# A chain of attention and feed-forward layers on one core: one low part placed ahead of a rotation, projections sent one slot later, and row sums by four narrow products

## The chip, the cores and the metric

The kernel runs on one core of a Trainium2 chip. The metric is the device time of one execution in microseconds (us). Each run of the kernel before is one such time; the profile is one further execution, recorded by the hardware profiler, with its own time and its own span from the first to the last instruction.

## What is computed

Four residual layers over x of shape (4, 1024, 256), each with a layernorm in front:

```python
x = x + attention0(layernorm(x))   # 8 heads of 64, keys and values from a 64-wide latent
x = x + ffn0(layernorm(x))         # 256 -> 1024 gated (silu), 1024 -> 1024 gelu, 1024 -> 1024 gelu, 1024 -> 256
x = x + attention1(layernorm(x))   # 16 heads of 16, rotary positions on q and k
x = x + ffn1(layernorm(x))         # 256 -> 768 gated (silu), 768 -> 256
# attention: softmax(q k^T * scale) v, and then the output projection
```

All is float32. A value that has to stay exact goes through TensorE in two parts: a high part rounded to fp32r, and a low part that holds what the rounding left. A low part is one elementwise subtraction.

## The kernel before

Two programs run one after the other. `attention_a` computes the first attention; `ffn_attention_ffn` computes the other three layers in one overlapped program. Each engine runs a written list of instructions in order; semaphores tie the lists together.

**First attention.** The work is cut into NU = 32 units (a batch, a pair of heads, a half of 512 queries), each of 8 steps of 128 keys; two steps make one turn, so that a unit has four turns j = 0 to 3. Within a turn TensorE computes row maxima (tile a_X, in three banks psX), scores (a_S), and the weighted values of the turn before (a_O, four products on 64 output partitions each). ScalarE takes the exponential (a_P), VectorE reduces the maxima (a_mraw) and adds some of the a_P tiles (a_accd), GpSimd adds the others (a_accp) and joins them. Once a unit, in turn j = 1, `sums(u - 1)` (L986 to L996) multiplies a block of ones with a_accd: two products, one for each head, each of 64 output partitions and 512 columns in full float32, so that the sum of the exponentials of each query stands 64 times in a bank. `keep_sums` (L591) copies the whole bank to `total`, `move_sums` (L468) spreads one row of each head with two transfers over the 128 partitions of `rcol`, 8 numbers each, `invert` (L740) takes the reciprocal in turn j = 2, and `move_inverse` sends it back through DRAM. The last unit keeps the wide form, because its reciprocals are taken straight from the bank.

**The program of the other three layers.** The first feed-forward works on NB = 8 batches k of 512 tokens; a batch has 64 slots H, and in each slot TensorE gets 5 or 6 of the 352 products of the batch (`slice_at`, `product`, L2005). They are grouped by output tile: 64 products make the 16 tiles gate and up, then come 8 tiles `("hidden", k, 0, m)`, 8 tiles `("hidden", k, 1, m)` and 2 tiles down, with 16 products a tile. ScalarE applies gelu twice for a hidden tile, once to a high part (act1h or act0h) and once to a full copy (m_xf); GpSimd's `low(key)` (L1926 to L1930) subtracts them into the low part (act1l or act0l). A product of the next layer reads high and low parts in turn over the 8 tiles m of the layer before; in `product` it waits by `s_lo`. So the first tile of the second hidden layer needs, with its fifteenth product, the low part of `("hidden", k, 0, 7)`, whose own last product stands in slot 34 of the batch.

Beside it runs the start of the second attention: for the batch kk = k - 1 that is through the feed-forward, `PROJECT` puts four projections (six products each, key and query in two halves) in slots 26, 30, 34 and 38, and `VALUES` four value products in slots 28, 32, 36 and 40. All use the one bank m_X. A projection is copied by ScalarE (`keep_projection`, tile m_qk, L1690), shuffled out of the bank by VectorE (`swap`, L1839), which waits for the end of the rotation before, rotated by GpSimd (`rotate`, three operations, L1938, L1940, L1942, result m_t1), rounded by ScalarE into the first half of the tile m_comp (`send_high`, L1696), its low part subtracted by GpSimd into the second half (`send_low`, L1947), and written to DRAM by SyncE's queue (`send`, L1513). There is one m_comp: `send_high` waits until the transfer of the projection before has landed (`s_sent`), and `rotate` waits for its low part.

What sets the order within a slot H is the loop of each engine. GpSimd: low parts of tiles up, `send_low`, output low parts, `rotate`, low parts of tiles hidden, the power of a layernorm. ScalarE: `keep_projection`, `send_high`, then the tiles that ended in this slot. `send_high` and `send_low` stand three slots after their projection, `send` five slots after it. START = 512 is the slot in which the second attention's scores begin; its first row maxima come 24 slots earlier, and the fourth query tile of the attention (index 3, used first by unit u = 5) is the tile m_comp, cleared by GpSimd's `fill_queries` at START + 46 and fetched at START + 48.

Of the kernel before, what the change touches and what calls it, by code (L numbers as in the profile page):

```python
# [10 lines left out]
ACT = mybir.ActivationFunctionType  # L11
# [113 lines left out]
def mm(pe, out, lhsT, rhs, start=True, stop=True):  # L125
    return pe.eng.matmul(out, lhsT, rhs, start=start, stop=stop, skip_group_check=True)  # L126
# [117 lines left out]
def attention_a(nc, x_in, x_out, weights, scales, c_ident, scratch, wtiles, wcopy, dtiles, dcopy, shared):  # L244
# [7 lines left out]
    NU = B * UB  # L252
# [93 lines left out]
    with ExitStack() as ctx:  # L346
# [15 lines left out]
        wo = [p.sb(f"wo{i}", [128, NG, 256], F32R) for i in range(2)]  # L362
        accd, accp = [p.sb(f"accd{i}", [128, NH, 512]) for i in range(2)], p.sb("accp", [128, NH, 512])
        mrow = [p.sb(f"mrow{i}", [NH * 4, 128], F32R) for i in range(2)]
        total = p.sb("total", [128, 512])
        wraw = p.sb("wraw", [128, NG, 320])
        rinv = [p.sb(f"rinv{i}", [128, 512]) for i in range(2)]
        ON = [p.sb(f"ON{i}", [128, NG, T]) for i in range(2)]
# [41 lines left out]
        def bank(key):  # L410
            return psX[:, X.slot(key), :]
# [24 lines left out]
        def sync(eng):  # L436
# [31 lines left out]
            def move_sums(u):  # L468
                sp.wait_ge(*X.emptied(("sums", u)))
                sp.wait_ge(s_rout, 16 * u)  # L470
                for h in range(NH):
                    sp.eng.dma_start(rcol[64 * h:64 * h + 64, :], total[64 * h:64 * h + 1, :]).then_inc(s_total, 16)

            def move_inverse(u):
                sp.wait_ge(s_rcol, u + 1)
# [65 lines left out]
        def scalar(eng):  # L541
# [49 lines left out]
            def keep_sums(u):  # L591
                key = ("sums", u)
                act.wait_ge(*X.filled(key))
                act.wait_ge(s_total, 32 * u)
                act.eng.activation(total[:, :], bank(key), ACT.Copy).then_inc(X.free(key))

            def out_high(b, t):
                i = out_index(b, t)
# [74 lines left out]
        def vector(eng):  # L673
# [64 lines left out]
                    dve.eng.tensor_tensor(acc[:, :, :], acc[:, :, :], P[n % NP][:, :, :], ALU.add).then_inc(s_addd)  # L738

            def invert(u):  # L740
                dve.wait_ge(s_total, 32 * (u + 1))
                dve.eng.reciprocal(rcol[:, :], rcol[:, :]).then_inc(s_rcol)

            def out_low(b, t):
# [163 lines left out]
        def tensor(eng):  # L908
# [77 lines left out]
            def sums(u):  # L986
                key = ("sums", u)
                pe.wait_free(X, key)
                pe.wait_ge(s_addp, 5 * u + (5 if u < NU - 1 else 4))
                pe.wait_ge(s_addd, 2 * u + 2)  # L990
                terms = (accd[u % 2],) if u < NU - 1 else (accd[u % 2], accp)
                for i, acc in enumerate(terms):
                    for h in range(NH):
                        ins = mm(pe, bank(key)[64 * h:64 * h + 64, :], ones[:, :], acc[:, h, :], i == 0, i == len(terms) - 1)
                ins.then_inc(X.full(key))

            def way(i):
# [97 lines left out]
def ffn_attention_ffn(nc, x_in, x_mid, x_att, x_out, attn, wcopy, dcopy, c_rope, scratch, shared):  # L1095
# [19 lines left out]
    NU = B * UB  # L1115
# [125 lines left out]
    def x_of(H, name):  # L1241
        x = x_at(H) if H >= 0 else None
        return x if x and x[0] == name else None
# [11 lines left out]
        return None  # L1255

    def send_at(H):
        return x_of(H - 5, "project")

    def send_high_at(H):  # L1260
        return x_of(H - 3, "project")

    def x_order():
        return [x_at(H) for H in range(END) if x_at(H)]
# [38 lines left out]
    with ExitStack() as ctx:  # L1303
# [155 lines left out]
        def sync(eng):  # L1459
# [144 lines left out]
            for H in range(END):  # L1604
                (k, s), h = divmod(H, SLOTS), H - START
                for i in weights_done_at(H - 1):
                    load_weights(i + 3)
                if H == LAST - 12:
                    load_norm(norm_of["d", 1])
                if H > LAST and H % 8 == 7 and last_at(H)[0] + 2 < NB:  # L1610
                    load_norm(norm_of["d", last_at(H)[0] + 2])
                for x in residuals_at(H - 1):
                    store(x)
                if x_of(H - 1, "rows"):
                    move_rows(x_at(H - 1)[1])
                if x_of(H - 1, "values"):
                    send_values(*x_at(H - 1)[1:])
                if send_at(H):
                    send(*send_at(H)[1:])
                gi, u = (h + 32) // 32, (h + 38) // 16  # L1620
                if (h + 32) % 32 == 0 and 0 <= gi < B * NG:
                    fetch_key(gi)
                if (h + 32) % 16 == 0 and 0 <= (h + 32) // 16 < 6:
                    fetch_query((h + 32) // 16)
                if (h + 38) % 16 == 0 and 6 <= u < NU:
                    fetch_query(u)
                if ended_unit_at(H, SUMS) is not None:
                    move_sums(ended_unit_at(H, SUMS))
                if ended_unit_at(H, INVERSES) is not None:
                    move_inverses(ended_unit_at(H, INVERSES))  # L1630
                    move_heads(ended_unit_at(H, INVERSES))
                if ended_unit_at(H, SPREAD) is not None:
                    spread_inverses(ended_unit_at(H, SPREAD))
                b, t = (h + 12) // 128, (h + 12) % 128 // 2
                if h % 2 == 0 and 0 <= b < B and t < NT:
                    fetch_values(b, t)
                if s == C_LOAD and 1 <= k <= NB:
                    load_norm(norm_of["c", k - 1])
                if s == B_LOAD and 1 <= k and k + 1 < NB:
                    load_norm(norm_of["b", k + 1])  # L1640
                if s == 46 and 1 <= k < NB:
                    load_rope(k)
                if H == START + 2:
                    for i in range(3):
                        load_last_gates(i)
                if H == START + 80:
                    load_last_back()
                if H == D_LOAD:
                    load_norm(norm_of["d", 0])
                for x in residuals_at(H + 7):  # L1650
                    if x[0] == "out":
                        load_residual(x)
                for x in residuals_at(H + 3):
                    if x[0] != "out":
                        load_residual(x)
# [266 lines left out]
        def gpsimd(eng):  # L1922
# [49 lines left out]
                    pool.eng.memset(f32(comp[64 * h + 32:64 * h + 64, :, :]), 0.0).then_inc(s_qfill)  # L1972

            for H in range(END):
                if H == START + 46:
                    fill_queries()
                for key in ended_at(H - 1):
                    if key[0] == "up":
                        low(key)
                if send_high_at(H):  # L1980
                    send_low(*send_high_at(H)[1:])
                if split_at(H):
                    out_low(*split_at(H))
                if ended_unit_at(H, NORMALISE) is not None:
                    b, g, half = unit(ended_unit_at(H, NORMALISE))
                    if g % 2:
                        normalise(b, g // 2, half)
                if x_of(H, "project"):
                    rotate(*x_at(H)[1:])
                for key in ended_at(H):  # L1990
                    if key[0] == "hidden":
                        low(key)
                if last_pair_at(H - 1):
                    last_low(*last_pair_at(H - 1))
                if norm_at(H) and norm_at(H)[1] == 0:
                    norm.power(pool, norm_at(H)[0])
                if H == C_PIECES[1]:
                    norm.power(pool, norm_of["c", NB - 1])
                if H == D_PIECES[1]:
                    norm.power(pool, norm_of["d", 0])  # L2000
# [268 lines left out]
```

## Time and profile before

| | us |
|---|---|
| median of 3 runs | 2463.66 |
| lowest and highest run | 2458.45, 2463.93 |
| time of the profiled execution | 2452.89 |
| span of the profiled execution | 2451.1 |
| mean granted clock of TensorE | 0.987 |

| engine | busy us | share of the span |
|---|---|---|
| TensorE (PE) | 2352.9 | 96% |
| its weight loads (PEld) | 1458.9 | 60% |
| VectorE (DVE) | 1508.7 | 62% |
| ScalarE (ACT) | 1352.8 | 55% |
| GpSimd (POOL) | 1044.7 | 43% |

A record of the profile gives the start of an instruction in us from the span's start, its duration, engine, line, operation, and the tiles that it writes and reads. Idle time stands in brackets with the engine and line that ended it. Matmuls are pipelined: the recorded duration of one reaches into the next, so what one occupies is read from the distance between two starts. The span falls into three stages: the first attention up to about 800 us, the first feed-forward from about 855 to 1570 us, and the second attention with the last feed-forward behind it.

### The profile page before, as it was taken

How to read it: one execution, taken by the hardware profiler on the slowest of the kernel's cores; microseconds unless marked ns; L12 is line 12 of the kernel's file. 1: busy time of each engine (PE TensorE's matmuls, PEld its weight loads, DVE VectorE, ACT ScalarE, POOL GpSimd, SP SyncE). 2: the span in 40 equal slices, each digit the busy share in tenths (PEclk: the TensorE clock that was granted, in tenths of full speed). 3: DMA queues.
4: the chain of work that ended last, by engine and by line, in shares of the span. 5: the costliest groups of instructions: out<-in, count | busy, mean ns of one | idle time of the engine just before them, and what ended most of it. 6: DMA issues, size and time to landing. Idle time of an engine off the chain costs nothing. (4 is left out here: it accounts for less than half of the span.)

```text
span 2451.1 us, 38790 instructions
## 1 busy us (share of the span) xinstructions
PE 2352.9 (96%) x15141; PEld 1458.9 (60%) x15141; DVE 1508.7 (62%) x1934; ACT 1352.8 (55%) x1787; POOL 1044.7 (43%) x674
## 2 busy tenths in 40 slices
PE   6989999999999899999999999999999999999899
PEld 4545555555555687877877877544444444444598
DVE  6887777777774223322222222689989989889364
ACT  3555555554454444444444444378878778778643
POOL 1656766766677346556456456130010000000354
PEclk8999999999999999999999999999999999999999
DMA  1211321221212455555555555533432333332232
GB/s 50 71 68 53 96 78 53 96 74 48 73 42 68 139 170 172 170 181 182 175 180 183 169 180 181 148 96 73 90 88 64 89 77 73 90 79 50 61 113 82
DMA packets 157702, 259.02 MB, mean 106 GB/s; under 512 B 37872, under 2 KB 98160, under 8 KB 157168
## 3 DMA queue, kind: packets, MB, share of 16 engines
q1 hardware_dynamic: 157520, 256.53, 34.9%
q8 instruction: 122, 2.00, 0.3%
q14 instruction: 60, 0.49, 0.1%
HBM read 206.52 MB, written 60.68 MB: 109 GB/s over the span
## 5 line engine op out<-in xcount | busy, mean ns | idle before, releaser
L1825 DVE TENSOR_REDUCE m_mraw<-m_R 128x2 f32<-128x1024 f32 x512 | 622.5, 1221 | 70.2 <-PE m_R L126 58.5
L1676 ACT ACTIVATE m_P<-m_R 128x1024 f32<-128x1024 f32 x512 | 524.1, 1025 | 151.6 <-PE m_R L126 151.3
L581 ACT ACTIVATE a_P<-a_S 128x1024 f32<-128x1024 f32 x256 | 248.9, 1024 | 208.3 <-PE a_S L126 208.3
L126 PE MATMUL m_O<-m_P,m_V 128*17 128x256 f32 x4096 | 330.5, 394 | 4.5 <-ACT m_P L1676 2.6
L1930 POOL TENSOR_TENSOR m_act0l<-m_xf,m_act0h 128x512 fp32r<-128x512 f32 x128 | 164.6, 1289 | 240.2 <-ACT m_xf L1738 136.3
L879 POOL TENSOR_TENSOR a_accp<-a_accp,a_P 128x1024 f32<-128x1024 f32 x96 | 250.9, 2614 | 15.2 <-ACT a_P L581 6.4
L126 PE MATMUL a_O<-a_P,a_V 128*64 128x512 f32 x1024 | 247.7, 605 | 4.5 <-ACT a_ON L589 4.5
L126 PE MATMUL m_R<-m_act0h,wt 128*128 128x512 f32 x640 | 251.4, 393 | 0.0
L712 DVE TENSOR_REDUCE a_mraw<-a_X 128x2 f32<-128x1024 f32 x164 | 200.0, 1219 | 82.9 <-PE a_X L126 82.9
L126 PE MATMUL m_R<-m_act0l,wt 128*128 128x512 f32 x640 | 250.4, 391 | 0.0
L126 PE MATMUL m_R<-m_act1h,wt 128*128 128x512 f32 x512 | 203.0, 397 | 12.3 <-POOL m_act1l L1930 12.3
L126 PE MATMUL m_R<-m_act1l,wt 128*128 128x512 f32 x512 | 203.6, 398 | 0.0
L126 PE MATMUL m_R<-m_Q,m_K 64*128 64x512 f32 x800 | 201.0, 499 | 2.3 <-DVE m_mraw L1825 2.0
L126 PE MATMUL m_R<-next_hi,wt 128*128 128x512 f32 x448 | 179.2, 400 | 13.8 <-issue 10.1
L126 PE MATMUL m_R<-m_K,m_Q 48*128 48x512 f32 x800 | 181.9, 450 | 4.3 <-ACT m_P L1676 2.2
L1954 POOL TENSOR_TENSOR m_ON<-m_ON,m_yt 128x512 f32<-128x512 f32 x16 | 20.5, 1281 | 383.5 <-DMA m_yt<-inverses 383.5
L126 PE MATMUL m_R<-next_lo,wt 128*128 128x512 f32 x448 | 178.6, 399 | 0.0
L126 PEld LDWEIGHTS m_O<-m_P,m_V 128*17 128x17 f32 x4096 | 85.2, 120 | 140.8 <-issue 131.2
L126 PEld LDWEIGHTS m_R<-m_Q,m_K 64*128 64x128 f32 x800 | 74.8, 183 | 151.7 <-issue 122.3
L126 PEld LDWEIGHTS m_R<-m_act0h,wt 128*128 128x128 f32 x640 | 120.2, 188 | 26.8 <-POOL m_act0l L1930 2.1
L126 PEld LDWEIGHTS m_R<-m_act0l,wt 128*128 128x128 f32 x640 | 120.3, 188 | 24.4 <-issue 0.5
L126 PE MATMUL a_X<-a_Kh,a_Qh 64*128 64x512 f32 x496 | 113.6, 449 | 18.3 <-DVE a_mraw L712 10.8
(244 smaller groups left out, 4264.2 us busy)
## 6 DMA issues: line engine op xcount, KB each, us to landing
wt<-wcopy SPq DMA_DIRECT2D x176, 512.0 KB, 3.4
m_xres<-x SPq DMA_DIRECT2D x96, 128.0 KB, 3.0
m_K<-bounce_k SPq DMA_DIRECT2D x96, 128.0 KB, 5.2
m_ln_x<-x SPq DMA_DIRECT2D x23, 512.0 KB, 4.2
a_tile<-in_L_ffn_tiles SPq DMA_DIRECT2D x22, 512.0 KB, 4.7
wcopy<-in_L_ffn_tiles SPq DMA_DIRECT2D x22, 512.0 KB, 5.4
m_Q<-bounce_q SPq DMA_DIRECT2D x150, 64.0 KB, 2.3
x<-m_xres SPq DMA_DIRECT2D x64, 128.0 KB, 2.7
```

The lines of the kernel that those rows point to most:

```text
L126: return pe.eng.matmul(out, lhsT, rhs, start=start, stop=stop, skip_group_check=True)
L581: act.eng.activation(P[n % NP][:, :, :], psS[n % 2][:, :, :], ACT.Exp, scale=SCALE).then_inc(s_exp)
L712: dve.eng.tensor_reduce(mraw[u % 2][:, t, :], psX[:, first:first + 2, :], AX.X, ALU.max).then_inc(X.free(key))
L879: pool.eng.tensor_tensor(accp[:, :, :], accp[:, :, :], P[n % NP][:, :, :], ALU.add).then_inc(s_addp)
L1676: act.eng.activation(P[h % 4][:, :, :], pair(key)[:, :, :], ACT.Exp, scale=SCALE).then_inc(R.free(key))
L1825: dve.eng.tensor_reduce(mraw[u % 2][:, at, :], pair(key)[:, :, :], AX.X, ALU.max).then_inc(R.free(key))
L1930: pool.eng.tensor_tensor(act_buf[dst][1][:, m, :], xf[fs(key) % 2][:, :], f32(act_buf[dst][0][:, m, :]), ALU.subtract).then_inc(s_lo)
L1954: pool.eng.tensor_tensor(ON[:, f, cols], ON[:, f, cols], yt[half][:, :], ALU.mult).then_inc(s_norm[half])
```

## The change

In the first attention, the sums of 31 of the 32 units are made by four products of 32 output partitions and 256 columns; product i takes half of the queries of one head. The bank then holds 256 columns, `total` has half its width and its copy too, and one transfer takes the rows 0, 32, 64 and 96 in place of two transfers of one row each.

In the first feed-forward, `send_high`, `send_low` and `send` stand one slot later. In GpSimd's slot, the low part of the tile `("hidden", k, 0, 7)` comes ahead of the rotation. At the start of the second attention, m_comp is cleared at START + 48 and the query of unit 5 fetched into it at START + 50.

```diff
-                for h in range(NH):
-                    sp.eng.dma_start(rcol[64 * h:64 * h + 64, :], total[64 * h:64 * h + 1, :]).then_inc(s_total, 16)
+                sp.eng.dma_start(rcol[:, :], total[0:128:32, :]).then_inc(s_total, 16)
...
-                act.eng.activation(total[:, :], bank(key), ACT.Copy).then_inc(X.free(key))
+                act.eng.activation(total[:, :], bank(key)[:, 0:256], ACT.Copy).then_inc(X.free(key))
...
-                terms = (accd[u % 2],) if u < NU - 1 else (accd[u % 2], accp)
-                for i, acc in enumerate(terms):
-                    for h in range(NH):
-                        ins = mm(pe, bank(key)[64 * h:64 * h + 64, :], ones[:, :], acc[:, h, :], i == 0, i == len(terms) - 1)
+                if u < NU - 1:
+                    for i in range(4):
+                        ins = mm(pe, bank(key)[32 * i:32 * i + 32, 0:256], ones[:, 0:32], accd[u % 2][:, i // 2, 256 * (i % 2):256 * (i % 2) + 256])
...
     def send_at(H):
-        return x_of(H - 5, "project")
+        return x_of(H - 6, "project")
...
     def send_high_at(H):
-        return x_of(H - 3, "project")
+        return x_of(H - 4, "project")
...
-                if (h + 32) % 16 == 0 and 0 <= (h + 32) // 16 < 6:
+                if (h + 32) % 16 == 0 and 0 <= (h + 32) // 16 < 5:
                     fetch_query((h + 32) // 16)
+                if h == 50:
+                    fetch_query(5)
...
-                if H == START + 46:
+                if H == START + 48:
                     fill_queries()
...
+                awaited = [key for key in ended_at(H) if key[0] == "hidden" and key[2:] == (0, MT - 1)]
+                for key in awaited:
+                    low(key)
                 if x_of(H, "project"):
                     rotate(*x_at(H)[1:])
                 for key in ended_at(H):
-                    if key[0] == "hidden":
+                    if key[0] == "hidden" and key not in awaited:
                         low(key)
```

TensorE's list in the first attention, at one unit's sums (a_O the weighted values, a_accd the added exponentials, a_Kh and a_Qh the parts of keys and queries; the shape is that of the output):

```order
@@ -122,5 +122,5 @@
 L126 MATMUL a_X<-a_Kh,a_Qh 128x512 x2
 L126 MATMUL a_O<-a_P,a_V 64x512 x4
-L126 MATMUL a_X<-a_accd,a_ones 64x512 x2
+L126 MATMUL a_X<-a_accd,a_ones 32x256 x4
 L126 MATMUL a_X<-a_Kh,a_Qh 128x512 x2
 L126 MATMUL a_S<-a_Qh,a_Kh 128x512 x2
```

The sums stay between the weighted values and the maxima; four products stand where two were.

GpSimd's list in a batch of the first feed-forward, slots 30 to 38, before (m_act1l are low parts of the first hidden layer, m_act0l of the second, m_t1 and m_t2 the rotation, m_comp the low part of what is sent):

```order
L1938 TENSOR_TENSOR m_t1<-m_qk,m_rope 128x512
L1940 TENSOR_TENSOR m_t2<-m_t2,m_rope 128x512
L1942 TENSOR_TENSOR m_t1<-m_t1,m_t2 128x512
L1930 TENSOR_TENSOR m_act1l<-m_xf0,m_act1h 128x512
L193 TENSOR_TENSOR m_ln_rstd<-m_ln_ve,m_ln_minus_half 128x4
L1947 TENSOR_TENSOR m_comp<-m_t1,m_comp 128x512
L1938 TENSOR_TENSOR m_t1<-m_qk,m_rope 128x512
L1940 TENSOR_TENSOR m_t2<-m_t2,m_rope 128x512
L1942 TENSOR_TENSOR m_t1<-m_t1,m_t2 128x512
L1930 TENSOR_TENSOR m_act1l<-m_xf1,m_act1h 128x512
L1947 TENSOR_TENSOR m_comp<-m_t1,m_comp 128x512
L1930 TENSOR_TENSOR m_act0l<-m_xf0,m_act0h 128x512
```

And now:

```order
L1942 TENSOR_TENSOR m_t1<-m_qk,m_rope 128x512
L1944 TENSOR_TENSOR m_t2<-m_t2,m_rope 128x512
L1946 TENSOR_TENSOR m_t1<-m_t1,m_t2 128x512
L1934 TENSOR_TENSOR m_act1l<-m_xf0,m_act1h 128x512
L193 TENSOR_TENSOR m_ln_rstd<-m_ln_ve,m_ln_minus_half 128x4
L1951 TENSOR_TENSOR m_comp<-m_t1,m_comp 128x512
L1934 TENSOR_TENSOR m_act1l<-m_xf1,m_act1h 128x512
L1942 TENSOR_TENSOR m_t1<-m_qk,m_rope 128x512
L1944 TENSOR_TENSOR m_t2<-m_t2,m_rope 128x512
L1946 TENSOR_TENSOR m_t1<-m_t1,m_t2 128x512
L1934 TENSOR_TENSOR m_act0l<-m_xf0,m_act0h 128x512
L1951 TENSOR_TENSOR m_comp<-m_t1,m_comp 128x512
```

The last low part of the first hidden layer has passed the three operations of the rotation; the low part of the sent projection still stands ahead of both, but belongs to slot 34 now.

ScalarE's list in slots 33 to 38, before (m_qk is the copy of a projection, m_comp the high part of what is sent, m_act1h and m_xf the two outputs of a hidden tile):

```order
L1696 ACTIVATE m_comp<-m_t1 128x512
L1690 ACTIVATE m_qk<-m_X 128x512
L1737 ACTIVATE m_act1h<-m_R,scol 128x512
L1738 ACTIVATE m_xf1<-m_R,scol 128x512
L1703 ACTIVATE m_vstage0<-m_X 128x256
L1696 ACTIVATE m_comp<-m_t1 128x512
L1737 ACTIVATE m_act0h<-m_R,scol 128x512
L1738 ACTIVATE m_xf0<-m_R,scol 128x512
L1690 ACTIVATE m_qk<-m_X 128x512
```

And now:

```order
L1694 ACTIVATE m_qk<-m_X 128x512
L1700 ACTIVATE m_comp<-m_t1 128x512
L1741 ACTIVATE m_act1h<-m_R,scol 128x512
L1742 ACTIVATE m_xf1<-m_R,scol 128x512
L1707 ACTIVATE m_vstage0<-m_X 128x256
L1741 ACTIVATE m_act0h<-m_R,scol 128x512
L1742 ACTIVATE m_xf0<-m_R,scol 128x512
L1694 ACTIVATE m_qk<-m_X 128x512
L1700 ACTIVATE m_comp<-m_t1 128x512
```

The high part of a sent projection stood ahead of the next projection's copy and stands behind it now, directly ahead of the hidden tile that ends in slot 34.

## Rows read from the trace of the kernel before

**Rows 1.** The page: busy time, share and instructions of TensorE and its weight loads.

```profile
PE 2352.9 (96%) x15141; PEld 1458.9 (60%) x15141; DVE 1508.7 (62%) x1934; ACT 1352.8 (55%) x1787; POOL 1044.7 (43%) x674
```

**Rows 2.** Who TensorE waited for: total us, times, longest.

```profile
PE m_R L126 <- POOL m_act1l L1930: 12.3, 7, 1.9
...
PE m_X L126 <- DVE m_t L1839: 0.9, 1, 0.9
```

**Rows 3.** Stretches: busy PE, PEld, DVE, ACT, POOL, granted clock, DMA share, GB/s.

```profile
200.00:300.00 100.00, 99.98 (x626) 56.48 (x624) 74.51 (x85) 49.91 (x62) 70.76 (x31) 1.00 0.28 90
...
1045.92:1050.92 5.00, 5.00 (x15) 3.98 (x16) 0.59 (x2) 2.27 (x4) 3.11 (x3) 0.66 0.59 209
...
1236.07:1241.07 5.00, 5.00 (x23) 4.17 (x24) 0.74 (x2) 2.20 (x4) 4.11 (x4) 1.00 0.62 209
```

**Rows 4.** TensorE in order of time at the wait of batch k = 2.

```profile
1043.39 0.39 PE L126 MATMUL m_R<-m_act1h,wt 128*128 128x512 f32 x1
1043.62 0.39 PE L126 MATMUL m_R<-m_act1l,wt 128*128 128x512 f32 x1
1045.92 0.50 PE L126 MATMUL m_R<-m_act1h,wt 128*128 128x512 f32 x1 [1.91 <-POOL m_act1l L1930]
...
1047.31 0.63 PE L126 MATMUL m_X<-next_lo,m_wqh 128*128 128x512 f32 x1
1047.74 0.63 PE L126 MATMUL m_X<-next_hi,m_wql 128*128 128x512 f32 x1
```

**Rows 5.** The same wait in batches 4 and 5.

```profile
1236.07 0.50 PE L126 MATMUL m_R<-m_act1h,wt 128*128 128x512 f32 x1 [1.91 <-POOL m_act1l L1930]
1329.56 0.60 PE L126 MATMUL m_R<-m_act1h,wt 128*128 128x512 f32 x1 [1.91 <-POOL m_act1l L1930]
```

**Rows 6.** ScalarE, VectorE and GpSimd in order of time, batch 2, slots 30 to 38.

```profile
1031.91 0.60 ACT L1690 ACTIVATE m_qk<-m_X 128x512 f32<-128x512 f32 x1 [0.67 <-PE m_X L126]
...
1039.00 0.60 ACT L1690 ACTIVATE m_qk<-m_X 128x512 f32<-128x512 f32 x1 [1.31 <-PE m_X L126]
...
1039.64 0.74 DVE L1839 STREAM_SHUFFLE m_t<-m_X 128x512 f32<-128x512 f32 x1
...
1040.65 1.29 POOL L1938 TENSOR_TENSOR m_t<-m_qk,m_rope 128x512 f32<-128x512 f32 x1
1040.72 0.68 ACT L1738 ACTIVATE m_xf<-m_R,scol 128x512 f32<-128x512 f32 x1
...
1044.55 1.31 POOL L1930 TENSOR_TENSOR m_act1l<-m_xf,m_act1h 128x512 fp32r<-128x512 f32 x1
1045.70 0.63 ACT L1696 ACTIVATE m_comp<-m_t 128x512 fp32r<-128x512 f32 x1 [3.11 <-DMA bounce_q<-m_comp]
```

**Rows 7.** The transfers of the tile m_comp, from issue to landing.

```profile
DMA to landing us min/median/max: 2.1/2.6/5.6
```

**Rows 8.** ScalarE in batch 7, ahead of the copy of the last projection.

```profile
1521.77 0.63 ACT L1696 ACTIVATE m_comp<-m_t 128x512 fp32r<-128x512 f32 x1 [5.34 <-DMA bounce_q<-m_comp]
```

**Rows 9.** TensorE in the first attention at one unit's sums.

```profile
404.72 1.03 PE L126 MATMUL a_X<-a_accd,a_ones 128*64 128x512 f32 x4
...
405.68 0.50 PE L126 MATMUL a_X<-a_Kh,a_Qh 64*128 64x512 f32 x2
```

**Rows 10.** TensorE in the second attention: four narrow products, and what follows.

```profile
1900.99 0.64 PE L126 MATMUL m_O<-m_P,m_V 128*17 128x256 f32 x8
1901.57 0.49 PE L126 MATMUL m_R<-m_Q,m_K 64*128 64x512 f32 x2
```

**Rows 11.** Sums of an early unit, and a wait behind them.

```profile
94.69 1.03 PE L126 MATMUL a_X<-a_accd,a_ones 128*64 128x512 f32 x4
96.34 0.50 PE L126 MATMUL a_X<-a_Kh,a_Qh 64*128 64x512 f32 x2 [0.62 <-DVE a_mraw L712]
```

**Rows 12.** The query of unit 5: its fetch on the queue, and its first use.

```profile
1652.38 2.96 SPq L1536 DMA_DIRECT2D m_comp<-bounce_q  x6
...
1664.29 0.50 PE L126 MATMUL m_R<-m_K,m_comp 48*128 48x512 f32 x2
```

More of the change, by code:

```diff
@@ L364, in attention_a @@
         mrow = [p.sb(f"mrow{i}", [NH * 4, 128], F32R) for i in range(2)]
-        total = p.sb("total", [128, 512])
+        total = p.sb("total", [128, 256])
         wraw = p.sb("wraw", [128, NG, 320])
@@ L593, in keep_sums @@
                 act.wait_ge(*X.filled(key))
-                act.wait_ge(s_total, 32 * u)
-                act.eng.activation(total[:, :], bank(key), ACT.Copy).then_inc(X.free(key))
+                act.wait_ge(s_total, 16 * u)
+                act.eng.activation(total[:, :], bank(key)[:, 0:256], ACT.Copy).then_inc(X.free(key))
             def out_high(b, t):
@@ L740, in invert @@
             def invert(u):
-                dve.wait_ge(s_total, 32 * (u + 1))
+                dve.wait_ge(s_total, 16 * (u + 1))
                 dve.eng.reciprocal(rcol[:, :], rcol[:, :]).then_inc(s_rcol)
@@ L990, in sums @@
                 pe.wait_ge(s_addd, 2 * u + 2)
-                terms = (accd[u % 2],) if u < NU - 1 else (accd[u % 2], accp)
-                for i, acc in enumerate(terms):
-                    for h in range(NH):
-                        ins = mm(pe, bank(key)[64 * h:64 * h + 64, :], ones[:, :], acc[:, h, :], i == 0, i == len(terms) - 1)
+                if u < NU - 1:
+                    for i in range(4):
+                        ins = mm(pe, bank(key)[32 * i:32 * i + 32, 0:256], ones[:, 0:32], accd[u % 2][:, i // 2, 256 * (i % 2):256 * (i % 2) + 256])
+                else:
+                    for i, acc in enumerate((accd[u % 2], accp)):
+                        for h in range(NH):
+                            ins = mm(pe, bank(key)[64 * h:64 * h + 64, :], ones[:, :], acc[:, h, :], i == 0, i == 1)
                 ins.then_inc(X.full(key))
```

## The prediction

> **What bounds the kernel now.** I read the page first, for the engine that is busy all the time: TensorE, 2352.9 of 2451.1 us [rows 1]. A change pays here only if it takes work or waiting from TensorE. Next comes the table of who TensorE waited for. In the first feed-forward it names one thing: seven waits, 12.3 us together, each ended by GpSimd's line 1930, the low part of a first-hidden-layer tile; a single wait of 0.9 us on the shuffle of the projection bank stands beside it [rows 2]. Third, stretches of time, where the reader should look at the granted clock. A hundred us of the first attention hold 99.98 us of TensorE work at 1.00, while the 5 us behind the second of the seven waits have a clock of 0.66 [rows 3]. Last, the timelines of the engines, to see what the waiting product waits for.
>
> What one of the seven waits costs: the starts at 1043.39 and 1043.62 are 0.23 us apart, those at 1043.62 and 1045.92 are 2.30 apart, so 2.07 us are lost (the bracket calls 1.91 of them idle). Behind it the starts lie 0.43 us apart, for products that took 0.23 before [rows 4]: the clock is at 1.2 in place of 2.4 GHz. From batch 2's wait to batch 4's are 190.15 us, 95.08 a batch [rows 4, 5]; from batch 4's to batch 5's 93.49 [rows 5], and behind batch 4's the clock stayed at 1.00 [rows 3]. The half clock thus costs 95.08 - 93.49 = 1.6 us. The granted clock fell so behind five of the six waits of 1.91 us (the stretches behind batches 1, 3, 5 and 6 repeat the 0.66 of batch 2); the seventh, 12.3 - 6 x 1.91 = 0.8 us idle [rows 2], was too short.
>
> **The low part ahead of the rotation.** The awaited low part needs m_xf, ready at 1040.72 + 0.68 = 1041.40. The three operations of the rotation began at 1040.65, so it started at 1044.55 and ended at 1045.86 [rows 6]; TensorE went on at 1045.92. TensorE wanted it at 1043.62 + 0.23 = 1043.85. Where does the new order put it? Everything that is moved counts here, since send_low of the projection before now stands in this slot too:
> - Slot 30: the projection's copy ends at 1031.91 + 0.60 = 1032.51 [rows 6]; send_high behind it 0.63, send_low 1.29, so to 1034.4. The transfer then waits its turn on SyncE's queue and lands at most 5.6 us after its issue [rows 7], at 1040.2 with 0.2 for the issue.
> - Slot 34: the copy of the projection ends at 1039.60 [rows 6], the transfer lets send_high run from 1040.2 to 1040.8, the two gelus take 0.68 each, to 1042.2, and send_low goes beside them, to 1042.1. The low part runs from 1042.2 to 1043.5.
>
> That is 0.3 us before TensorE wants it, with the slowest transfer of the trace. The wait goes, and the half clock behind it. Six waits give 6 x 2.07 = 12.4 us and the seventh about 1.0; the clock gives 5 x 1.6 = 8.0. Together **21.4 us**.
>
> What is late next: the rotation of slot 34 starts at 1043.5 instead of 1040.65. GpSimd then has the low part of the second hidden layer, send_low and the next rotation in front of it, but no product reads those low parts before the layer is through. The shuffle of projection 38 waits for the rotation's end, 1043.5 + 3.9 = 1047.4, and the value product of slot 40 waits for the shuffle. Slot 38's projection, starting at about 1044.8 without the wait (1047.31 is its second product, already at the low clock [rows 4]), ends at 1046.2; eleven products of 0.23 put the value product at 1048.7, against 1047.4 + 0.74 for the shuffle [rows 6]. It holds, by 0.5 us.
>
> **The projections sent a slot later.** In batch 7 send_high stood ahead of the copy of the last projection and sat idle for 5.34 us until a transfer had landed [rows 8], and TensorE waited 0.9 us for the shuffle behind it [rows 2]. With the copy ahead, that goes: **0.9 us**. In the other batches the same idle time (3.11 us [rows 6]) hid behind TensorE's work and is worth nothing. The later transfers pass a weight load on SyncE's queue; weights are loaded three tiles ahead, and no wait for them is in the table, so nothing. At the start of the second attention the fetch for unit 5 moves from slot START + 48 to + 50, some 2.7 us (1664.29 - 1652.38 = 11.9 us lay between its issue at + 48 and its use after + 56 [rows 12]). Its six issues take 2.96 us and land within 5.6, so 2.7 + 2.96 + 5.6 = 11.3 of 11.9 us: nothing, with little to spare at the longest landing and 3.5 us at the usual one.
>
> **The sums.** From the start of the sums to that of the next product: 405.68 - 404.72 = 0.96 us [rows 9]. The nearest row to the new form are the second attention's four products of 256 columns, side by side on four strips of 32 partitions, 0.58 us [rows 10]. Both must hold a part that goes with the columns and a fixed part for leaving the form: P + s = 0.96 and P/2 + s = 0.58 give P = 0.76 and s = 0.20. If going from the 64-wide products of a_O to 32-wide ones is free, a unit saves 0.38 us; if it costs another s, 0.18. I take half of it, 0.28. The Trainium skill (TensorEngine Tiling (Array Packing), Key Properties) says that changing the tiling mode drains TensorE, which speaks against this edit: by that rule it is 0.18. No row of the trace changes between two such forms, so neither is shown.
>
> 31 units have the new form. Five of them come within 2 us before a wait for VectorE (1.65 us in [rows 11]), or for the copy of the sums, which then only grows; elsewhere, as in [rows 3], TensorE is the bound and the gain stays. 26 x 0.28 = **7.3 us**, between 26 x 0.18 = 4.7 and 31 x 0.38 = 11.8. The narrower copy and the single transfer are off the path: ScalarE and the queue are idle there, and the reciprocal comes a turn later.
>
> **The sum:** 21.4 + 0.9 + 7.3 = 29.6 us. Against the profiled execution, 2452.9 - 29.6 = 2423.3. The median of the runs is 10.8 us above that execution; carried to it, **2434.0 us**, which is what I predict.
>
> **The rivals.**
> - *The wait comes back in part.* The awaited low part now hangs on ScalarE's send_high, and so on a landing. For it: the margin is 0.3 us, and the row of batch 7 shows such a landing late. Against: the longest landing is in my sum already. One us late in each batch would leave 7 us of waiting and about half of the clock's 8: 11 us of the gain, **2445**.
> - *The narrow sums give nothing.* If the change of form costs s on the way in and more on the way out, 26 x 0.28 is gone: **2441**. For it stands the rule above; against it the 0.58 us.
> - *Slower.* Same place as the first: if the landing comes so late that the low part ends later than before. It decides from 1045.86 on; to be slower by 7.4 us (0.3%) the 7.3 us of the sums must be lost too, so (7.4 + 7.3)/7 = 2.1 us later still, at 1048. The transfer would have to take 10 us; the longest took 5.6. **2472**.
> - *The change doesn't do what it says.* The low part is earlier but TensorE then stops at the next shared thing, the projection bank: rotation, shuffle, value product, with 0.5 us of margin. If each batch lost 2 us and some clock there, little is left with the sums at their low end: **2459**.
>
> **How the numbers follow.** My forecast gets 0.71, the rivals in their order 0.11, 0.10, 0.03 and 0.05. The range must hold 8 in 10. Below: all clock falls of un-profiled runs gone (six instead of five) and 0.38 us for each sum, from the lowest run: 2458.5 - (13.4 + 9.6 + 0.9 + 11.8) = 2423, rounded to 2422. Above, it takes in the first two rivals with a little for scatter, 2448. A measurement of this kernel tells apart about 0.3%, 7.4 us. Faster by more: 0.92 (the forecast and the first two rivals); within it: 0.05; slower: 0.03.
>
> **What would show it.** In the changed profile the row of waits on GpSimd's low part of m_act1h should be gone or under 1 us, and the batches 91.3 to 91.5 us apart; the granted clock in the feed-forward should be 1.00 throughout; send_low, low part, rotation should follow each other without the rotation in front. In the first attention, sums should occupy 0.6 to 0.8 us up to the next start. If the batches are still above 93 us, my chain of slot 34 is wrong; if sums take 0.96 or more, the part on the narrow products is.

## The result, and the profile after

| | before | changed |
|---|---|---|
| median of the runs, us | 2462.36 (4 runs) | 2427.49 (4 runs) |
| lowest and highest run, us | 2458.45, 2463.93 | 2424.36, 2434.60 |
| profiled execution: time, span, us | 2452.89, 2451.1 | 2428.58, 2426.7 |
| mean granted clock in it | 0.987 | 0.988 |

The ratio of the times is 0.9865, with a 95% interval of 0.9839 to 0.9890: faster by 34.9 us in the medians, by 27 to 40 in the interval, and by 24.3 us from one profiled execution to the other. To see where those 24 us lie, I read the starts of five products on TensorE: the first sums, the last sums, the first product of the feed-forward, and the first and last weighted values of the second attention.

| stretch, us | before | changed | difference | predicted |
|---|---|---|---|---|
| start, to the first sums | 72.9 | 74.7 | +1.8 | 0 |
| first attention, first to last sums | 715.0 | 704.7 | -10.3 | -7.3 |
| from there to the first product of the feed-forward | 23.1 | 28.1 | +5.0 | 0 |
| feed-forward, to the first weighted value | 764.3 | 742.1 | -22.2 | -22.3 |
| second attention, first to last weighted value | 720.6 | 722.0 | +1.4 | 0 |
| end | 155.2 | 155.1 | -0.1 | 0 |

The row of the profile's page that answers to [rows 1]: 15 us less busy TensorE, with 124 more products.

```profile
PE 2337.8 (96%) x15265; PEld 1454.2 (60%) x15265; DVE 1512.7 (62%) x1934; ACT 1344.9 (55%) x1787; POOL 1046.1 (43%) x674
```

**The feed-forward.** Who TensorE waited for between 855 and 1575 us, longest first. Both rows of [rows 2] belong here: the 12.3 us for the low part are gone, and of the shuffle's wait 0.5 us are there, at another place. The 1.7 us for m_P lie at the start of the second attention, at 1548 us; the kernel before has them too (1.75 us, at 1574).

```profile
PE m_R L126 <- ACT m_P L1680: 1.7, 1, 1.7
PE m_X L126 <- DVE m_t L1843: 0.5, 1, 0.5
PE m_R L126 <- DMA wt<-wcopy: 0.3, 1, 0.3
```

Stretches of time, columns as in [rows 3]: the feed-forward from 860 to 1530 us and 5 us in it, both at the full clock. In the kernel before the first of these stretches held 656.78 us of TensorE work at 0.99.

```profile
860.00:1530.00 670.00, 669.20 (x3086) 546.56 (x3084) 199.29 (x366) 302.75 (x488) 377.85 (x298) 1.00 0.56 182
1043.00:1048.00 5.00, 5.00 (x23) 4.13 (x22) 0.00 (x0) 2.48 (x5) 4.92 (x5) 1.00 0.81 245
```

The first product of the key projection in slot 26 of three batches is 91.26 and 91.27 us from the next, where [rows 4, 5] have 95.08 and 93.49:

```profile
1198.77 0.39 PE L126 MATMUL m_X<-next_hi,m_wkh 128*128 128x512 f32 x1
...
1290.03 0.39 PE L126 MATMUL m_X<-next_hi,m_wkh 128*128 128x512 f32 x1
...
1381.30 0.39 PE L126 MATMUL m_X<-next_hi,m_wkh 128*128 128x512 f32 x1
```

The same slots of batch 2 as in [rows 6], on ScalarE, GpSimd and VectorE. The copy of slot 34's projection starts here at 1031.99, there at 1039.00: the whole batch is 7.01 us earlier.

```profile
1031.99 0.60 ACT L1694 ACTIVATE m_qk<-m_X 128x512 f32<-128x512 f32 x1 [3.05 <-PE m_X L126]
...
1032.78 0.63 ACT L1700 ACTIVATE m_comp<-m_t 128x512 fp32r<-128x512 f32 x1 [0.19 <-DMA bounce_k<-m_comp]
...
1033.64 1.29 POOL L1951 TENSOR_TENSOR m_comp<-m_t,m_comp 128x512 fp32r<-128x512 f32 x1
...
1033.89 0.68 ACT L1742 ACTIVATE m_xf<-m_R,scol 128x512 f32<-128x512 f32 x1
...
1034.88 1.35 POOL L1934 TENSOR_TENSOR m_act1l<-m_xf,m_act1h 128x512 fp32r<-128x512 f32 x1
...
1036.20 1.33 POOL L1942 TENSOR_TENSOR m_t<-m_qk,m_rope 128x512 f32<-128x512 f32 x1
...
1038.91 1.28 POOL L1946 TENSOR_TENSOR m_t<-m_t 128x512 f32<-128x512 f32 x1
...
1040.30 0.01 DVE L1843 LOAD_MASK_SELECT m_t<-m_X  x1 [1.32 <-POOL m_t L1946]
...
1040.33 0.76 DVE L1843 STREAM_SHUFFLE m_t<-m_X 128x512 f32<-128x512 f32 x1
```

The order is the one that the lists promised: copy, high part (it sat idle 0.19 us for the landing of the transfer before), gelus, low part of what is sent, the awaited low part at 1034.88, and only then the rotation. And TensorE at the two places where it could have stopped:

```profile
1036.61 0.39 PE L126 MATMUL m_R<-m_act1l,wt 128*128 128x512 f32 x1
...
1036.84 0.39 PE L126 MATMUL m_R<-m_act1h,wt 128*128 128x512 f32 x1
...
1041.37 0.28 PE L126 MATMUL m_X<-m_wvh,next_hi 128*128 128x256 f32 x1
```

1036.84 is the product in front of which stood 1.91 us of idle time in [rows 4]; its low part ended at 1034.88 + 1.35 = 1036.23, 0.61 us earlier. The value product at 1041.37 starts 0.28 us after the end of the shuffle, 1040.33 + 0.76 = 1041.09.

In batch 1 this second place did become a wait. The rotation had ended at 948.14, but VectorE was still busy with a memset until 949.16, and the shuffle began only then:

```profile
947.40 1.76 DVE L1859 MEMSET m_K<- 32x2048 f32 x1 [0.48 <-issue]
...
949.21 0.74 DVE L1843 STREAM_SHUFFLE m_t<-m_X 128x512 f32<-128x512 f32 x1
...
950.00 0.39 PE L126 MATMUL m_X<-m_wvh,next_hi 128*128 128x256 f32 x1 [0.52 <-DVE m_t L1843]
```

**The sums.** TensorE at an early unit, as in [rows 11], and at one in the middle, as in [rows 9]:

```profile
94.29 1.94 PE L126 MATMUL a_O<-a_P,a_V 128*64 128x512 f32 x8
96.15 0.64 PE L126 MATMUL a_X<-a_accd,a_ones 128*32 128x256 f32 x8
97.78 0.50 PE L126 MATMUL a_X<-a_Kh,a_Qh 64*128 64x512 f32 x2 [0.99 <-DVE a_mraw L711]
...
401.85 0.64 PE L126 MATMUL a_X<-a_accd,a_ones 128*32 128x256 f32 x8
402.42 0.50 PE L126 MATMUL a_X<-a_Kh,a_Qh 64*128 64x512 f32 x2
```

From the sums to the next product it is now 0.57 us in place of 0.96, but from the weighted values to the sums it is 1.86. In the kernel before that distance was 1.77, from the row below to the sums at 404.72 [rows 9]:

```profile
402.95 1.94 PE L126 MATMUL a_O<-a_P,a_V 128*64 128x512 f32 x8
```

So a unit saves 0.39 us and pays 0.09 to 0.10 on the way in: 0.29 to 0.30.

### The profile page after: what moved, and what is told of

It is laid out like the page before. It is cut to its first block and busy times, and to the rows that moved or that the text cites. A ratio compares the mean times of both kernels' runs of the same rounds, so it can differ in the third digit from the quotient of the medians.

```text
span 2426.7 us, 39031 instructions
## 1 busy us (share of the span) xinstructions
PE 2337.8 (96%) x15265; PEld 1454.2 (60%) x15265; DVE 1512.7 (62%) x1934; ACT 1344.9 (55%) x1787; POOL 1046.1 (43%) x674
## 5 line engine op out<-in xcount | busy, mean ns | idle before, releaser
L126 PE MATMUL m_R<-next_hi,wt 128*128 128x512 f32 x448 | 179.0, 400 | 17.9 <-issue 14.2
L126 PEld LDWEIGHTS m_R<-m_act0l,wt 128*128 128x128 f32 x640 | 120.3, 188 | 24.3 <-issue 0.5
```

## The experiments

My theory: the feed-forward's 22 us are the seven waits and the half clock behind them, the low part's place brings them, and the sums bring the rest. The rivals: it is the later sending that matters, or the sums gain nothing because the change of form is paid for. And there was one thing that I hadn't foreseen, the 5 us ahead of the feed-forward. The four kernels of the first group ran on one chip, beside 23 runs of the kernel before with a median of 2456.58.

### The sums alone

```diff
+                    for i in range(4):
+                        ins = mm(pe, bank(key)[32 * i:32 * i + 32, 0:256], ones[:, 0:32], accd[u % 2][:, i // 2, 256 * (i % 2):256 * (i % 2) + 256])
```

with the narrow copy and the one transfer.

> Only the four narrow products with their copy and transfer. Theory (sums cost 0.57 us to the next start plus 0.10 us more ahead of them, against 0.96 before): 0.29 us a unit, of which five units keep nothing: 7 to 9 us under the kernel before, ratio 0.9965, and the feed-forward keeps its seven waits. Rival (the 10.3 us that the first attention gained in the changed kernel's profile come from elsewhere, such as the phase of VectorE's waits): less than 4 us.

Measured: 2448.31 us (12 runs), ratio 0.9972 [0.9957, 0.9987], 8.3 us faster. The first attention took 706.9 us, the stretch behind it 28.0, the feed-forward 764.5. The sums thus bring about what the units say, and the extra 5 us ahead of the feed-forward come with them. By these two stretches the sums would be worth 3 us, the lower end of what the interval of the runs allows. Whether the 5 us are lost in the runs without the profiler too stays open (below, under "Between the programs").

### The feed-forward part alone

```diff
-        return x_of(H - 3, "project")
+        return x_of(H - 4, "project")
...
+                for key in awaited:
+                    low(key)
                 if x_of(H, "project"):
                     rotate(*x_at(H)[1:])
```

with `send_at` and the query of unit 5.

> Only the feed-forward's part: the awaited low part ahead of the rotation and the projections a slot later. Theory (seven waits, five half clocks, one wait for the shuffle): 22 us under the kernel before, ratio 0.991, batches 91.3 us apart. Rival (the 35 us between the medians are mostly this part, since un-profiled runs of the kernel before have more half clock than its profile): 25 us or more.

Measured: 2436.58 us (6 runs), ratio 0.9928 [0.9903, 0.9952], 20.0 us faster. The feed-forward took 743.1 us, the stretch ahead of it 24.2. The two parts give 28.3 us together, 5 to 7 us less than the whole change in its two measurements; that is within the noise of differences between medians here. In the profiles the parts add up stage by stage: the feed-forward lasts about as long as with the whole change (742.1), the first attention with the sums alone about as long (704.7). That the two parts act on each other isn't shown.

### The awaited low part ahead, the sends where they were

```diff
+                for key in awaited:
+                    low(key)
                 if x_of(H, "project"):
                     rotate(*x_at(H)[1:])
```

> Only the awaited low part ahead of the rotation; send_high, send_low and send stay three and five slots behind their projection. Theory (the low part alone takes the waits away; the later sends only save batch 7's wait for the shuffle): within 2 us of the kernel with the whole feed-forward part, low part at the gelu's end + 1.3 us. Rival (without the later sends the transfer's landing holds up ScalarE and the shuffle, so waits come back at the value product of slot 40): waits of 1 us or more in each batch, 8 to 15 us slower than the whole part.

Measured: 2447.61 us (12 runs), ratio 0.9972 [0.9957, 0.9987], only 9.0 us faster; the feed-forward took 754.0 us. Who TensorE waited for in it:

```profile
PE m_X L126 <- DVE m_t L1839: 9.8, 7, 2.0
```

Seven waits again, but for the shuffle. The timeline of batch 2 shows why, on all four engines:

```profile
1040.63 1.28 POOL L1930 TENSOR_TENSOR m_act1l<-m_xf,m_act1h 128x512 fp32r<-128x512 f32 x1 [1.03 <-ACT m_xf L1738]
...
1045.81 0.63 ACT L1696 ACTIVATE m_comp<-m_t 128x512 fp32r<-128x512 f32 x1 [4.13 <-POOL m_t L1942]
...
1047.49 0.60 ACT L1690 ACTIVATE m_qk<-m_X 128x512 f32<-128x512 f32 x1
...
1048.12 0.73 DVE L1839 STREAM_SHUFFLE m_t<-m_X 128x512 f32<-128x512 f32 x1
...
1048.91 0.38 PE L126 MATMUL m_X<-m_wvh,next_hi 128*128 128x256 f32 x1 [1.28 <-DVE m_t L1839]
```

The low part is early (1040.63) and so the rotation is late. ScalarE's `send_high` waits 4.13 us for it, and in this kernel the next projection's copy stands behind `send_high`: 1047.49. The shuffle waits for the copy, and the value product for the shuffle. In the full change the copy comes first. So my theory, which gave the later sends 2 us at most, falls, and the rival stands: without them the new order gives 11.0 of its 20.0 us back at the projection bank. Behind this wait the granted clock stayed at its upper level:

```profile
1048.91:1053.91 5.00, 5.00 (x25) 4.28 (x26) 0.00 (x0) 2.29 (x4) 4.92 (x5) 1.00 0.63 215
```

### The sends later, the low part where it was

```diff
-        return x_of(H - 3, "project")
+        return x_of(H - 4, "project")
```

and `send_at` and the query of unit 5 with it.

> Only the projections a slot later, the awaited low part still behind the rotation. Theory (send_low now stands ahead of the rotation in slot 34 and pushes it and the low part back by 1.3 us or more): the seven waits grow from 1.9 to about 3.3 us, 8 to 10 us slower than the kernel before, ratio 1.004. Rival (the later sends are what frees the queue): waits unchanged or shorter, same time as before or faster.

Measured: 2476.75 us (6 runs), ratio 1.0099 [1.0074, 1.0123], 20.2 us slower, twice what I expected; the rival, that the later sends are what frees the queue, is out. The feed-forward took 779.7 us. Who TensorE waited for in it, twice the 12.3 us of [rows 2]:

```profile
PE m_R L126 <- POOL m_act1l L1932: 24.6, 7, 4.0
```

Batch 2 on ScalarE, GpSimd and TensorE:

```profile
1038.80 0.60 ACT L1692 ACTIVATE m_qk<-m_X 128x512 f32<-128x512 f32 x1 [3.05 <-PE m_X L126]
...
1039.62 0.63 ACT L1698 ACTIVATE m_comp<-m_t 128x512 fp32r<-128x512 f32 x1 [0.22 <-DMA bounce_k<-m_comp]
...
1040.45 1.29 POOL L1949 TENSOR_TENSOR m_comp<-m_t,m_comp 128x512 fp32r<-128x512 f32 x1
...
1041.88 1.29 POOL L1940 TENSOR_TENSOR m_t<-m_qk,m_rope 128x512 f32<-128x512 f32 x1
...
1045.75 1.31 POOL L1932 TENSOR_TENSOR m_act1l<-m_xf,m_act1h 128x512 fp32r<-128x512 f32 x1
...
1047.12 0.79 PE L126 MATMUL m_R<-m_act1h,wt 128*128 128x512 f32 x1 [3.31 <-POOL m_act1l L1932]
```

`send_low` stood ahead of the rotation in the kernel before as well, so its place in the list isn't what my theory took it for. What moved is the time from which it can run. `send_high` now follows the copy of slot 34's projection (1038.80) and ends at 1040.25; in the kernel before it had ended at 1037.68, ahead of that copy:

```profile
1037.05 0.63 ACT L1696 ACTIVATE m_comp<-m_t 128x512 fp32r<-128x512 f32 x1 [1.10 <-POOL m_t L1942]
```

Counted from the start of the copy, the rotation begins after 3.08 us, where [rows 6] have 1.65. It is 1.43 us later, and the wait grew by 1.40, from 1.91 to 3.31. The 5 us behind the wait ran wholly at the low clock, where [rows 3] have 0.66:

```profile
1047.00:1052.00 5.00, 4.88 (x12) 3.82 (x13) 0.00 (x2) 1.90 (x4) 1.34 (x2) 0.50 0.32 105
```

The feed-forward is 15.4 us longer: 12.3 us are waiting, of which I had counted 8 to 10, and the rest is more time at the low clock, which I had left out. The profiled execution is the quickest of the six, with a mean granted clock of 0.985; the four slowest have 0.980 to 0.982, so the other 5 us are probably more low clock; where it lay isn't shown.

Alone the two edits are worth -9.0 and +20.2 us, together -20.0. The low part's new place brings less than half without the later sends, and the later sends without it only cost.

### What the change of form costs: wide columns, narrow strips

```diff
+                        width = 32 if u < NU - 1 else 64
-                        ins = mm(pe, bank(key)[64 * h:64 * h + 64, :], ones[:, :], acc[:, h, :], i == 0, i == len(terms) - 1)
+                        ins = mm(pe, bank(key)[64 * h:64 * h + width, :], ones[:, 0:width], acc[:, h, :], i == 0, i == len(terms) - 1)
```

> The kernel before with its two products of the sums on 32 instead of 64 output partitions, still of 512 columns each, same number of instructions. Theory (0.10 us are paid ahead of the sums because the width of the strips changes after a_O, and what a unit saves goes with the columns): the first product of the sums comes 1.87 us after a_O instead of 1.77, and the sums still take 0.96 us to the next start. Rival (the width itself sets the time): under 0.9 us to the next start. Idle time at the change of program 10.1 us, as in the kernel before, since no instruction is added.

Measured: one execution of 2461.12 us beside 2458.47. TensorE at one unit's sums:

```profile
404.56 1.94 PE L126 MATMUL a_O<-a_P,a_V 128*64 128x512 f32 x8
406.43 1.05 PE L126 MATMUL a_X<-a_accd,a_ones 128*32 128x512 f32 x4
407.41 0.50 PE L126 MATMUL a_X<-a_Kh,a_Qh 64*128 64x512 f32 x2
```

Two products of 512 columns on 32 output partitions: from the weighted values 1.87 us, to the next product 0.98. The way in has the 0.10 us of the changed kernel, with the columns of the kernel before. The 0.10 us thus come with going from 64 to 32 output partitions, and the gain comes from the columns that each product takes, 256 in place of 512: 0.98 down to 0.57. The first attention took 721.6 us, longer than the units explain (31 x 0.12 = 3.7). In this profile TensorE waited for VectorE twice, for 2.14 and 1.87 us, with more than 3 us at the low clock from about 599 and from about 755 us, where the kernel before stayed at the full clock.

### The narrow sums twice

```diff
-                    for i in range(4):
+                    for i in (0, 1, 2, 3, 0, 1, 2, 3):
```

> The changed kernel with the four narrow products of 31 units made twice. Theory (a second set of four costs 0.43 us and TensorE is the bound in all but some five units): the first attention from the first sums to the last is 11 us longer than the 704.7 us of the changed kernel, at most 13.5. Rival (VectorE's waits hide more than that): under 8 us.

Measured: one execution of 2432.94 us. The sums at the same unit:

```profile
401.90 1.07 PE L126 MATMUL a_X<-a_accd,a_ones 128*32 128x256 f32 x16
402.90 0.50 PE L126 MATMUL a_X<-a_Kh,a_Qh 64*128 64x512 f32 x2
```

1.00 us for eight products, 0.57 for four: 0.43 for four more. Over 31 units that is 13.3 us; the first attention took 716.7 us, 12.0 longer than in the changed kernel and 10.6 longer than the average of six such profiles (below), which lie between 703 and 709 us. That is over the rival's 8 us and speaks for most units passing on what their sums cost or save; how many, one profile can't tell.

### Between the programs

The 5 us ahead of the feed-forward lie in one idle stretch of TensorE between the two programs, in which it waited for nothing that the profile shows. With the narrow sums the list of TensorE's instructions is longer. The trace records the loading of instructions as a queue of its own, in blocks of 16 KB. I thought that the place at which a program ends within a block decides how many are loaded in the gap, and moved it, by two or eight more products in one unit (their results are written over by the same values):

```diff
-                    for i in range(4):
+                    for i in (0, 1, 0, 1, 2, 3) if u == 0 else range(4):
```

and `3 * (0, 1, 2, 3)` for the larger one.

> The changed kernel with two of the narrow products of the first unit repeated, eight instructions more for TensorE in the whole first attention. Theory (the idle time between the two programs is set by how many 16 KB blocks of TensorE's instructions have to be loaded there, two in the kernel before and three in the changed one, so by the place of the program's end in a block; the narrow products added 248 instructions and a block may hold 256): two blocks and 10.1 us idle instead of 14.2, 3 to 4 us faster than the changed kernel. Rival (what the narrow products cost there has nothing to do with blocks): 14.2 us as before.

> The changed kernel with eight more narrow products in the first unit, 32 instructions. Theory of the blocks: two blocks and 10.1 us idle, if the eight instructions of the kernel with two repeats were too few as well as if they were enough; 3 to 4 us faster than the changed kernel less 0.9 us for the products. Rival: 14.2 us idle, and 1 us slower than the changed kernel.

The changed kernel: TensorE's first product of the feed-forward, and the instruction queue in the 17 us that end with it (packets, MB, share):

```profile
807.47 0.59 PE L126 MATMUL m_R<-next_hi,wt 128*128 128x512 f32 x1 [14.19 <-issue]
```

```profile
q8 instruction: 2, 0.03, 0.8%
```

The kernel with two more products, the same two views:

```profile
807.18 0.80 PE L126 MATMUL m_R<-next_hi,wt 128*128 128x512 f32 x1 [10.31 <-issue]
```

```profile
q8 instruction: 1, 0.02, 0.4%
```

One block less, and 3.9 us less idle time. In the changed kernel the two loads start at 800.91 and 804.92 us, 4.0 us apart, and the product comes 2.55 us after the second; here the only load starts 2.56 us ahead of the product. (The three and two blocks of the expectations count one more, which is loaded just behind that product.) All twelve profiles of this study agree: two blocks in those 17 us and 14.0 to 14.2 us idle in the changed kernel (both profiles) and with the sums alone; one block and 9.5 to 10.3 us in the other nine. The medians do not follow: 2427.85 us (ratio 0.9873 [0.9854, 0.9892]) and, with eight products, 2428.33 (0.9882 [0.9862, 0.9901]), beside 2458.47 for the kernel before. So I ran the changed kernel and the one with two products once more, on one chip.

> The changed kernel once more, on the same chip as the two-repeat kernel. Theory of the blocks: again three blocks and 14.2 us idle between the programs, with the first attention between 704 and 710 us, since its length from profile to profile scatters by some 2 us to both sides.

> The changed kernel with two narrow products repeated in the first unit, on the same chip as the changed kernel. Theory of the blocks: two blocks, 10.3 us idle, and a median 3 to 4 us under that of the changed kernel beside it. Rival (the shorter idle time is given back by the first attention, which was 708.7 and 709.3 us in the two padded kernels and 704.7 in the changed one): medians within 1 us.

Measured: 2426.02 us (5 runs, ratio 0.9863 [0.9843, 0.9883]) for the changed kernel, 2428.54 (6 runs, 0.9882 [0.9861, 0.9902]) with two products more, beside 2459.23. In the profiles the gap is again 14.0 and 10.0 us. The intervals overlap and the order of the medians is the wrong one. That the shorter gap makes the kernel faster is not shown; the runs of one of these kernels lie up to 13 us apart, and what hides 4 us in them, or takes them back, stays open. No version here beats the changed kernel.

## Why the prediction was right, and where it wasn't

**The low part ahead of the rotation** was predicted at 21.4 us and the later send of batch 7 at 0.9; the feed-forward lost 22.2. The chain of slot 34 holds in its parts. Counted from the copy of its projection, I had the low part end after 1043.5 - 1039.0 = 4.5 us and TensorE want it after 4.85; it ended after 1036.23 - 1031.99 = 4.24 and was wanted after 4.85. The landing came earlier than the longest of [rows 7], so the margin was 0.6 us in place of 0.3. The second margin was the tighter one, 0.28 us where I had 0.5: the shuffle ended where it should (after 9.10 us, predicted 9.14), but the value product came after 9.38 in place of 9.7. In batch 1 it was used up by a memset that I hadn't counted, and the wait came to 0.52 us. That part of the last rival is real, but small.

**The half clock** behind five of the waits is gone, as predicted, and the batches came to 91.26 us, just under the 91.3 to 91.5 that I had named.

**The projections sent later** is the step that was wrong in its reasons. I wrote that in the other batches the idle time "hid behind TensorE's work and is worth nothing". It is worth more than half of the feed-forward's gain: without the later sends the low part's new place brings 9.0 us, not 20, since the high part that waits for the late rotation then stands ahead of the next copy. I had priced the later sends in the order before, where the rotation is early. The sum was right only because the chain of slots 34 to 40 was worked out with both edits in it. The fetch for unit 5 was worth nothing, as predicted: issued at 1631.5, used at 1640.5, with no wait.

**The sums** were predicted at 0.28 us a unit, from 0.58 for the products and half of 0.20 for the change of form. Measured were 0.57 and 0.10. The Trainium skill's rule (TensorEngine Tiling (Array Packing), Key Properties) that a change of the tiling mode drains TensorE points the right way, and the trace agrees that there is a cost, with 0.10 us on the way in; it is half of what I had made of the rule. I had the right size by luck: 0.10 was the middle between two cases that I couldn't tell apart. How many units keep their gain was the weaker part: I said 26 of 31. The early unit above keeps none of it, with its wait for VectorE grown from 0.62 [rows 11] to 0.99 us. But TensorE's waits in the first attention (75 to 778 us) are 25.6 us together where they were 27.8, and the attention took 706.1 us on average in the six profiles with the narrow sums as in the change, 714.9 in the four with the sums of before. That is 8.8 us, close to 31 x 0.29 = 9.0, within the 4.7 to 11.8 that I gave.

**Missed: the gap between the programs**, 4.1 of the 5.0 us ahead of the feed-forward. No term of my sum stood for it.

**Against the median.** The sum, 29.6 us, put the profiled execution at 2423.3; it came to 2428.6, by the gap (+4), start and second attention (+3), less 3 from the sums. The median came to 2427.5, where I had 2434.0. The term that failed there is the 10.8 us by which I carried the sum from the profiled execution to the median: that execution was a quick one of the kernel before, and the changed kernel's median lies 1.1 us below its own. The difference of the medians was 34.9 us here and 33.2 in the repetition, against 28.3 for the two parts measured singly. My 29.6 lies within the interval; whether the surplus is real stays open.

**The rivals.** The wait came back in no batch at its old place, the narrow sums gave what they promised, and the slower case needed a transfer of 10 us where the longest took 6.0. What it feared does cost that much, though by another way than a late landing: the kernel with the sends alone has the low part 1.4 us later in its batch and is 20 us slower.

## What to carry to other kernels

When one operation is moved ahead of a chain on one engine, follow the chain once round the other engines in the new order, and price edits that touch the same chain together: here they are worth -9 and +20 us apart, and -20 joined. Take the clock behind a stall into its price, and look for the next shared buffer's margin, since the gain ends there. A profiled execution may lie at the edge of its runs: compare a sum with its own execution, and widen the range for the median.

## What the runs showed of the hardware

**Instruction blocks.** TensorE sat idle between two programs for about 10 us with one block of 16 KB loaded in the 17 us ahead of the next product, and for 14 us with two, whose loads start 4.0 us apart; two more products in one unit, 700 us earlier, were enough to go from two to one. The Trainium skill (Advanced Engine Details and Errata, ISA Cache) gives 16 KB as a line of the instruction cache; the trace agrees: the 39 packets of that queue up to the feed-forward's first product in the changed kernel are 0.64 MB together, 16 KB each.

**Waits and the clock.** In the feed-forward, six waits of 1.28 to 1.32 us left the granted clock at 2.4 GHz, five of six waits of 1.91 us were followed by some 3 us at 1.2 GHz, and one of 3.31 us by 5 us at 1.2 GHz throughout. But length alone doesn't tell. In the kernel with the sends alone the same wait in batch 1 lasted 3.35 us, in work at the full clock, and the clock stayed up:

```profile
952.16 0.50 PE L126 MATMUL m_R<-m_act1h,wt 128*128 128x512 f32 x1 [3.35 <-POOL m_act1l L1932]
```

```profile
952.16:957.16 5.00, 5.00 (x23) 4.20 (x24) 2.57 (x4) 2.38 (x4) 2.59 (x3) 1.00 0.34 108
```

And in the second attention, whose products had been running at the full clock, the second profile of the changed kernel has this wait for a transfer, and then, 3 us later, this stretch:

```profile
1746.20 0.50 PE L126 MATMUL m_R<-m_K,m_Q 48*128 48x512 f32 x2 [1.40 <-DMA m_K<-bounce_k]
```

```profile
1749.00:1754.00 5.00, 5.00 (x35) 1.49 (x27) 2.95 (x3) 2.84 (x5) 0.73 (x1) 0.52 0.11 30
```

In the first profile the same product waited 0.64 us and the clock stayed up. That stage took 728.6 us in the one and 722.0 in the other. Such waits for keys (0.9 to 4.9 us together in the twelve profiles, in kernels with and without the change) are one source of the scatter between executions of one kernel. How much of the time ran at the low clock goes with most of it: among the 23 runs of the kernel before that stood beside the first four experiments, the four with a mean granted clock of 0.989 took 2445.3 to 2452.5 us, and the two with 0.984 took 2458.0 and 2460.9.
